# A gated scan, local attention and a routed FFN on one core: earlier loads of x, and another order of steps in the first and last turns

## The reference

```
z = tanh(conv(W_z)); f = sigmoid(conv(W_f)); o = sigmoid(conv(W_o))     # two taps, 374 rows come out
c = f*c + (1-f)*z ;  h = o*c                                              # a scan over the rows
h = h + attn(layernorm(h))    # 8 heads of 16, 39 offsets back: 0..32, 48, 64, 96, 128, 192, 256
                              # per offset a product q*k summed over the head, softmax over offsets,
                              # weighted sum of v, times sigmoid(x@W_gate), times W_out
h = h + ffn(layernorm(h))     # router over 64 experts, top 2, at most 128 rows kept per expert
                              # gelu(x@w1.T)@w2.T, weighted by the probabilities of what was kept
```

## Time and profile before

| | us |
|---|---|
| median of 3 runs | 436.83 (436.8 to 437.9) |
| the profiled execution, its own time | 434.99 |
| its span in the trace | 433.2 |
| a full turn in the steady part (score to score on PE: 94.71, 119.58, 144.44) | 24.87 |

### The profile page before, as it was taken

One profiled execution on the slowest core, in us unless ns is written; L12 is line 12 of the kernel. 1 busy time (PEld: TensorE's weight loads), 2 busy tenths in 40 slices (PEclk: granted clock), 3 DMA queues, 4 the chain that ended last, 5 costly groups with the idle time before them and its releaser, 6 DMA issues.

```text
span 433.2 us, 12681 instructions
## 1 busy us (share of the span) xinstructions
PE 410.9 (95%) x4554; PEld 280.3 (65%) x4554; DVE 387.0 (89%) x873; ACT 323.6 (75%) x728; POOL 372.9 (86%) x389
## 2 busy tenths in 40 slices
PE   8789899999999999999999999999999999998884
PEld 5444364776757676776767677676757676766763
DVE  4487999899999999999999999999999999999563
ACT  3756677879687877968687887868788796858773
POOL 7596999999989989898998989898998999997611
PEclk9999899999999999999999999999999999999999
DMA  8330757452726365363726446182734537164500
GB/s 287 130 102 3 196 148 198 103 173 61 200 81 156 107 148 153 81 171 99 196 68 145 145 115 188 50 196 81 170 108 120 164 96 201 41 192 125 143 12 24
DMA packets 78703, 56.08 MB, mean 129 GB/s; under 512 B 28305, under 2 KB 71345, under 8 KB 78513
## 3 DMA queue, kind: packets, MB, share of 16 engines
q1 hardware_dynamic: 78640, 55.28, 47.2%
HBM read 35.56 MB, written 19.70 MB: 128 GB/s over the span
## 4 chain that ended last, share of the span: by engine, by line
PE 78%; DVE 11%; issue 4%; ACT 2%; DMA 2%; POOL 2%; SPq 0%; DVEq 0%; POOLq 0%; ACTq 0%
PE bank L450 20%; PE bank L539 9%; PE bank L516 8%; PE bank L400 6%; PE bank L426 6%; PE bank L401 5%; PE bank L478 5%; PE bank L466 4%; DVE prod L1228 4%; PE bank L458 3%; PE bank L508 2%; PE bank L493 2%; PE bank L418 2%; PE bank L434 2%; PE bank L411 1%
## 5 line engine op out<-in xcount | busy, mean ns | idle before, releaser
L1698 POOL TENSOR_TENSOR prod<-q,k 128x1496 f32<-128x1496 f32 x48 | 144.5, 3028 | 21.8 <-ACT k L852 16.1
L1228 DVE SCALAR_TENSOR_TENSOR prod<-bank,par,k 128x1496 f32<-128x1496 f32 x80 | 140.8, 1766 | 0.0
L450 PE MATMUL bank<-prod,ew 128*32 128x374 f32 x1024 | 87.3, 479 | 1.7 <-ACT gate L859 1.0
L1683 POOL TENSOR_TENSOR fprod<-q,k 128x374 f32<-128x374 f32 (+6 forms) x112 | 80.3, 753 | 0.0
L450 PEld LDWEIGHTS bank<-prod,ew 128*32 128x32 f32 x1024 | 31.3, 109 | 47.1 <-issue 41.1
L953 ACT ACTIVATE hid<-bank,par 128x374 f32<-128x374 f32 x64 | 36.3, 575 | 23.5 <-PE bank L516 21.7
L786 ACT ACT_TABLE_LOAD x40 | 51.3, 1283 | 1.4 <-PEq L1918 0.7
L516 PE MATMUL bank<-x,par 128*128 128x374 f32 x128 | 48.3, 483 | 1.9 <-ACT x L906 1.9
L539 PE MATMUL bank<-par,hid 128*128 128x128 f32 x384 | 47.9, 276 | 0.0
L539 PEld LDWEIGHTS bank<-par,hid 128*128 128x128 f32 x384 | 45.9, 192 | 2.6
L400 PE MATMUL bank<-xT,par 128*128 128x374 f32 x96 | 41.2, 511 | 3.7 <-DMA xT<-x_dram 3.1
(11 more groups left out here) (119 smaller groups left out, 876.8 us busy)
## 6 DMA issues: line engine op xcount, KB each, us to landing
band<-band_scratch SPq DMA_DIRECT2D x16, 768.0 KB, 5.2
band_scratch<-attn SPq DMA_DIRECT2D x64, 180.4 KB, 3.0
vnear<-v_scratch SPq DMA_DIRECT2D x48, 192.0 KB, 2.9
v<-v_scratch SPq DMA_DIRECT2D x32, 192.0 KB, 4.1
v_scratch<-vtok SPq DMA_DIRECT2D x16, 192.0 KB, 3.0
xT<-x_dram SPq DMA_DIRECT2D x16, 187.5 KB, 3.4
vfar<-v_scratch SPq DMA_DIRECT2D x16, 128.0 KB, 3.3
out_dram<-osb SPq DMA_DIRECT2D x16, 128.0 KB
```

Of the source, the lines that this page charges most:

```text
L450: done = mm(home(f"s{c}")[32 * g:32 * g + 32, lo:N], ew[:, c * CW + j, :], src[:, j, lo:N], start=first or only, stop=last or only)
L1228: v.scalar_tensor_tensor(bass.AP(prod[c][:, :, :].tensor, part * N, [[CW * N, 128], [PARTS * N, w], [1, N]]), home("q")[:, 0:N].unsqueeze( ...
L1683: last = g.tensor_tensor(fprod[:, i, o:N], q[q_.s][:, o:N], k[q_.s][:, KPAD:KPAD + N - o], ALU.mult)
L1698: g.tensor_tensor(bass.AP(prod[c][:, :, :].tensor, part * N, [[CW * N, 128], [PARTS * N, w], [1, N]]), q[q_.s][:, :].unsqueeze(1).broadcas ...
```

## The change

SP issues the loads of x for batch 1 ahead of the second piece of the parameters, and for batch 2 ahead of the clearing of the DRAM scratch. The steps of turns 0 to 6 and of turns 16 and later are written out in another order on all five engines. The loops shrink by a turn or two, so turn 6 and turn 16 (on PE turn 17) are now written out. No step is added or dropped, and no step's own code changes.

```diff
@@ SP @@
             load_x(Seq(0, 0, 0))
+            load_x(Seq(1, 1, 0))
             sp.dma_start(par[:, cut:PCOLS], params[:, cut:PCOLS]).then_inc(par_in, 16)
             sp.dma_start(prod[1][:, :, :].rearrange("p c n -> p (c n)")[:, 0:ALLCOLS - PCOLS],
                          params[:, PCOLS:ALLCOLS]).then_inc(par_in, 16)
-            load_x(Seq(1, 1, 0))
+            load_x(Seq(2, 0, 1))
 
             sp.wait_ge(pads_zero, 1)
...
             read_far(seq[15])
-            store_out(seq[11])
             write_attn(seq[15])
             read_values(seq[15])
             read_band(seq[15])
+            store_out(seq[11])
             store_out(seq[12])
@@ PE @@
             project(seq[0], "q")
-            convolve(seq[3], 0, ("z", seq[2]), head=True)
             convolve(seq[2], 2, ("k", seq[0]))
             value_project(seq[0], ("f", seq[2]))
+            project(seq[0], "g")
+            convolve(seq[3], 0, ("z", seq[2]), head=True)
             convolve(seq[3], 1, ("v", seq[0]))
             turn_h(seq[1], ("ht", seq[0]))
-            project(seq[0], "g")
...
             convolve(seq[4], 0, ("ts0", seq[0]), head=True)
+            convolve(seq[4], 1, ("v", seq[1]))
+            turn_h(seq[2], ("ht", seq[1]))
             project(seq[1], "g", ("ts2", seq[0]))
-            turn_h(seq[2], ("ht", seq[1]))
-            convolve(seq[4], 1, ("v", seq[1]))
@@ PE, the turn after batch 13's first scores @@
+            score(seq[13], 2, 0, ("s1", seq[13]), first=True)
+            score(seq[13], 0, 3, last=True)
+            turn_x(seq[14], ("op", seq[11]))
+            turn_band(seq[12], 0, ("v", seq[13]), head=True)
+            score(seq[13], 2, 1, last=True)
+            turn_scores(seq[13], 1, ("q", seq[13]))
@@ DVE @@
             recur_out(seq[1])
+            products(seq[0], 0, 1, head=True)
             recur_in(seq[2])
             recur(seq[2])
-            products(seq[0], 0, 1, head=True)
...
-            near_values(seq[0])
             products(seq[1], 1, 0)
...
             finish(seq[11])
-            softmax_sum(seq[13])
-            softmax_rcp(seq[13])
             score_add(seq[14], 1)
```

More of the change, by code:

```diff
@@ L684, in _ @@
             score(seq[2], 0, 2)
-            pipeline(pe, turn, range(6, 18))
+            score(seq[2], 2, 0, ("s1", seq[2]), first=True)
+            score(seq[2], 0, 3, last=True)
+            score(seq[2], 2, 1, last=True)
+            turn_scores(seq[2], 1, ("q", seq[2]))
+            turn_scores(seq[2], 0, ("s0", seq[2]))
+            turn_x(seq[3], ("op", seq[0]))
+            turn_x2(seq[0], ("ts0", seq[2]))
+            turn_band(seq[1], 0, ("f", seq[5]), head=True)
+            turn_band(seq[1], 2, ("tb2", seq[0]))
@@ new lines, in _ @@
+            down(seq[0], 1)
+            down(seq[0], 2)
+            score(seq[3], 1, 0, ("g", seq[3]), first=True)
+            score(seq[3], 1, 1)
+            score(seq[3], 1, 3)
+            score(seq[3], 1, 2, last=True)
+            score(seq[3], 0, 1, ("z", seq[6]), first=True)
+            score(seq[3], 0, 0)
+            score(seq[3], 0, 2)
+            pipeline(pe, turn, range(7, 17))
+            score(seq[13], 2, 0, ("s1", seq[13]), first=True)
+            score(seq[13], 0, 3, last=True)
@@ new lines, in _ @@
+            positions(seq[11], ("up2", seq[11]))
+            out_project(seq[12], ("up0", seq[11]))
+            down(seq[11], 0, ("lg", seq[11]), head=True)
+            down(seq[11], 1)
+            project(seq[14], "g", ("up1", seq[11]))
+            turn_h(seq[15], ("ht", seq[14]))
+            down(seq[11], 2)
+            score(seq[14], 1, 0, ("g", seq[14]), first=True)
+            score(seq[14], 1, 1)
+            score(seq[14], 1, 3)
+            score(seq[14], 1, 2, last=True)
+            score(seq[14], 0, 1, ("up3", seq[11]), first=True)
@@ new lines, in _ @@
+            tanh_z(seq[6])
+            tanh_f(seq[6])
+            router_exp(seq[0])
+            norm2_ln(seq[1])
+            norm1_ln(seq[4])
+            norm2_exp(seq[1])
+            norm1_exp(seq[4])
+            half_forget(seq[6])
+            softmax_exp(seq[2])
+            score_copy(seq[3], 1)
+            norm2_rows(seq[1])
+            norm1_rows(seq[4])
+            score_copy(seq[3], 0)
+            pipeline(act, turn, range(7, 16))
+            score_copy(seq[12], 2)
+            norm1_back(seq[13])
@@ L1520, in _ @@
             score_add(seq[2], 0)
-            pipeline(dve, turn, range(6, 17))
+            softmax_sum(seq[1])
+            softmax_rcp(seq[1])
+            score_add(seq[2], 2)
+            score_max(seq[2])
+            score_subtract(seq[2])
+            products(seq[3], 0, 1, head=True)
+            attention_sum(seq[1])
+            attention_norm(seq[1])
+            near_values(seq[2])
+            attention_gate(seq[1])
+            recur_out(seq[5])
+            route_max(seq[0])
+            route_picks(seq[0])
+            route_mask(seq[0])
+            products(seq[3], 1, 0)
+            residual(seq[1])
+            products(seq[3], 0, 2)
+            keep(seq[0])
+            stats2(seq[1])
+            stats1(seq[4])
+            recur_in(seq[6])
+            take_room(seq[0])
+            products(seq[3], 0, 0)
+            shift2_rows(seq[1])
+            shift_rows(seq[4])
+            products(seq[3], 0, 3)
+            gate_sum(seq[0])
+            add_b2(seq[0])
+            gate_weight(seq[0])
+            softmax_sum(seq[2])
+            recur(seq[6])
+            finish(seq[0])
+            score_add(seq[3], 1)
+            score_add(seq[3], 0)
+            pipeline(dve, turn, range(7, 17))
             score_add(seq[13], 2)
```

309 lines of the change are left out of this document (232 added, 77 removed).

## The result

| | before | after |
|---|---|---|
| median of the runs, us | 436.80 (435.43 to 437.90, 9 runs) | 438.38 (437.50 to 439.89, 9 runs) |
| profiled execution, own time, us | 434.99 | 437.50 |
| its span, us | 433.2 | 435.7 |

The ratio is 1.0041, with a 95% interval of 1.0026 to 1.0057: slower by 1.8 us, with an interval of 1.1 to 2.5 us. The time lies 1.2 us above the 437.2 that I forecast. "Same", my likeliest case, was not what came; the size of the loss is near that of the rival in which TensorE's clock falls at the new gap (438.6). That it is so near is in part luck, as the sum at the end shows.

A forecast was written before the change was run, and what follows sets the result against it. PE was taken to bound turns from 95 to 320, DVE 341 to 401, then a drain. Start -1.65, last turns +0.6 and store +1.45 gave +0.4 on the 436.83 median: 437.2 us, range 434.5 to 439.2.

The forecast's parts named there:

- "Same": Whole kernel: a change under 0.3% (1.3 us), which can hardly be told from none; chance 0.43.
- x of batch 1 and 2: Start: earlier loads end PE's waits of 0.86 and 2.20 us; POOL's first products come 1.1 us earlier.
- q and k of batch 1: Start: POOL begins batch 1 at 39.4 and not 39.98, 0.6 us won after 0.5 for PE's transposes.
- carry(0): Start: this 1.0 us step leaves POOL's gapless stretch for idle time; batch 2's products start 1.6 us earlier, at 59.35.
- The start, -1.65: Up to turn 6: PE 2.15 us ahead, less a 0.5 us wait; bounds -0.6 and -2.15.
- products(2, 0, 0), 0.47: Start: going ahead of two statistics, it removes PE's 0.47 us wait at 72.90.
- Given back in turn 6: POOL's part 1 of batch 3's far products ends at 98.85, PE asks at 98.3: PE waits 0.5 us.
- The order of the last turns, +0.6: End: transposes delay DVE by 0.4 and 0.5 us, moved softmax steps return 0.3; bounds -0.4 and +0.9.
- store_out(11), +1.45: End: the store, queued behind a 768 KB band read, holds finish(13) until 408.1; bounds 0 and +2.5 us.
- The band reads come late: Rival: value reads ahead of band reads on SP delay them about 0.9 us, giving +1.3, 438.1; chance 0.08.
- the clock rival: Start: TensorE's clock falls at PE's new gap of 22.0 to 24.6, taking 1.4 us: 438.6, slower; chance 0.15.

The follow-up runs named there:

- d2: The changed kernel with six idle matmuls, whose result nobody reads, in PE's new gap of 22.0 to 24.6; ratio 1.0028 to before.
- e3: The changed kernel's start with before's end, batch 0's band read in its old place and idle matmuls in both PE gaps of the start; ratio 0.9956 to before.
- c3: The changed kernel with only store_out(11) put back ahead of write_attn(15); ratio 1.0017 to before.
- d1: The kernel before with only store_out(11) moved behind the last band read, read_band(15); ratio 1.0067 to before.
- c4: The kernel before with only the loads of x of batches 1 and 2 moved up on SP; ratio 0.9969 to before.
- e4: The kernel before with the early loads of x and six idle matmuls in PE's gap ahead of project(1, "g"); ratio 0.9951 to before, 434.00 us.

## Why the prediction was right or wrong

*x of batch 1 and 2: right.* Forecast 9.15, 18.05, 21.45 and 21.4; the rows have 9.19, 17.96, 21.44 and (DVE) 21.31. PE's gap of "about 22.0 to 24.6" ended at 24.61, released by the scan.

*q and k of batch 1, carry(0): right only at full clock.* Forecast 39.4, 59.35 and 2.5 us ahead at batch 3; the changed kernel has 40.73, 60.66 and 81.60 (1.15 ahead). Counted from P0, the forecast says 17.95, 37.9 and 58.8. d2, whose clock did not fall before 46.8, has 17.79, 37.74 and 58.66.

*The start, -1.65: the step that failed is the clock.* Batch 3's first score is at 94.64 in before (22.57 + 72.07). The prediction has PE 2.15 ahead there, ahead of the wait that gives 0.5 back, so its s3 is 94.64 - 2.15 - 21.45 = 71.04. The changed kernel has 73.10, and e3, with full clock, 71.58. So 1.52 of the miss is the clock. The mechanism stood among the rivals with 0.15 and a price of 1.4; it came, and took 1.5. The prediction had named the sign itself: wrong if the clock drops after 24 or stays full after 45. Both happened. So the time lies in the range while the path that was to give it did not hold. I should have given the rival more: the new gap was nearly as long as the one that had such a sequel in the earlier trace rows. My reason for a low chance was the 2.20 us gap ahead of 16.52 that had none, and c3 shows that a gap may or may not have one. What I had not priced is that the stretch of the earlier trace rows would go away in exchange. That gives back little, since POOL covered it there.

*products(2, 0, 0), 0.47: the wait moved.* The other 0.54 of the miss in s3 is there at full clock too. PE's wait of 0.47 for the product is gone, but `turn_x2(0)` now waits for DVE's `score_add(2)`, 0.34 here and 0.43 in e3, where before has no wait:

```profile
76.86 0.55 PE L507 MATMUL bank<-par,xrow 128*128 128x128 f32 x3 [0.34 <-DVE sc L1420]
```

From batch 2's first score to batch 3's before needs 25.56, the changed kernel 25.63 and e3 25.72. So that term gave nothing.

*Given back in turn 6: it came, at 0.18 and not 0.5.* `kw` waited 0.49 for `exr` (forecast 0.2), and part 1 stood at 98.69 (forecast about 97.2) and ended at 100.34. PE's last score of batch 3 needs it:

```profile
99.59 0.81 PE L457 MATMUL bank<-prod,ew 128*32 128x374 f32 x8
100.40 0.62 PE L457 MATMUL bank<-fprod,ew 128*32 128x246 f32 x6
```

In before the second row follows the first by 0.63 (99.69, 100.32), here by 0.81. That is the +0.20 of the piece to batch 13's first score. In e3 the wait is 0.12. It is smaller than the forecast because PE was late itself.

*The order of the last turns, +0.6: direction right, size 1.07 up to `finish(13)` and 1.53 up to `finish(15)`.* DVE's wait behind `turn_band` was 0.73 and not 0.4: PE began `turn_scores(13)` at 348.57, 0.76 later than before, of which `turn_band` is 0.53 (347.50 to 348.03) and 0.10 the later start of the turn. A wait of 0.26 for `kw` was not on my list. `score_add(14)` did not wait, where I had expected 0.5: `softmax_sum(13)` and its reciprocal now run behind it, at 376.17. What that costs is not shown by itself.

*store_out(11), +1.45: the wait is right, the price is smaller.* The wait is 1.41. In the pair with c3 it costs 1.30 up to `finish(13)` and 0.85 up to `finish(15)`, so "nothing hides it" was wrong by 0.45. d1 shows the move costing by itself. The row that I went by (6.0 us from issue to the last packet behind the band read) gave the time; here it is 6.6 us, 402.54 to 409.12. The Trainium skill, DMA: Bandwidth & Descriptors, section Latency and other measured facts, has a fixed cost of about 2 us for a DMA; for a store queued behind a read of 768 KB no run here agrees with it. I missed that the wait leaves PE idle long enough for a low clock in the drain, which took 2.1 us in d1's trace.

*The band reads come late: true in part.* It had 0.08. The wait came in the start (0.20), not in the end.

*The sum.* -1.65 + 0.6 + 1.45 = +0.4 against +2.5 in the profiles. The start came to +0.10 at batch 13's first score and not -1.65, which is 1.75: the clock 1.52, the wait that moved and other small ones 0.54, less the 0.32 by which the wait in turn 6 was smaller. The end came to +2.4 and not +2.05: the order 0.93 more, the store 0.60 less. In the medians the loss is +1.6, because before's median execution is slower than the profiled one that I started from. So the forecast of 437.2 missed by 1.2 us and not by 2.1, and the clock rival's 438.6 was met almost exactly, by luck: my sum took the median to stand 1.84 over the profile after the change too, and it stands 0.9 over it.

## What to carry to other kernels

Price a new gap on TensorE by what may follow it: one of 2.4 us was meant to cost nothing itself and cost 1.5 us in slower matmuls behind it. Idle matmuls in this gap alone gave back 0.9 in the trace, since the clock then fell at the next gap; in both gaps they gave back 1.5. Before a store or read is moved down a DMA queue, ask who waits for its landing and how long the transfer ahead of it occupies the queue. And do the plain edit by itself: the two early loads alone were worth -0.31%, and everything else in the change, the new orders and the store, cost 0.7% on top of them (1.0041 against 0.9969).

## What the runs showed that I had not expected

The low clock comes behind one of a few gaps, and which one it is differs between executions of the same order of instructions: in the changed kernel at 25.2, behind the gap of 2.4 us; in c3, with the same start, at 47.8, behind one of 1.64 us. Its price depends on the place: 1.5 us where POOL waits for q and k behind it, 0.6 to 0.8 at 47 in the new order (s3 of d2 and c3 against e3), 0.3 at 45 in before's order (c4 against e4), 2.1 in the drain of d1, where it lasted twice as long. The traces of e3 and e4, whose long gaps are filled, have none while PE has matmuls.

A kernel's profiled execution need not be a typical one. Before's was 1.8 us faster than its median, and the mean granted clock goes with that: 0.994 in the profiled one, 0.990 or 0.991 in nearly all those around the median.
